# Graph attention on one core: masks turned two chunks at a time, statistics aggregated on GpSimd, another order at the end

## The reference

```python
h = maximum(layernorm(x), 0)                    # over the 256 features, eps 1e-5
Wh = h @ W                                      # 256 x 256
f1, f2 = Wh @ a[:256], Wh @ a[256:]
e = f1[:, :, None] + f2[:, None, :]
e = where(e >= 0, e, 0.2 * e)
att = softmax(where(adj > 0, e, -9e15), axis=1)
out = x + elu(einsum('bij,bjo->bio', att, Wh))
```

## Time and profile before

| | us |
|---|---|
| median of 3 runs | 989.29 |
| lowest, highest | 988.13, 992.64 |
| the profiled execution | 987.88 |
| its span | 986.1 |

### The profile page before, as it was taken

The page is one execution under the profiler, slowest core; times in us unless marked ns, Lnnn a source line. Parts: engine busy times, 40 slices in busy tenths (PEclk is TensorE's granted clock), DMA queues, the critical chain, the costliest instruction groups (busy, mean ns, idle before and its releaser), DMA issues.

```text
span 986.1 us, 23861 instructions
## 1 busy us (share of the span) xinstructions
PE 950.0 (96%) x8993; PEld 840.0 (85%) x8993; DVE 920.7 (93%) x1271; ACT 879.3 (89%) x1237; POOL 645.3 (65%) x676
## 2 busy tenths in 40 slices
PE   8878999999999999999999999999999999999996
PEld 6666888889888898888888888888988989898896
DVE  8799989999899998999989998999999999999975
ACT  4788989999999999999999899999999999898985
POOL 6567665776766776876767776677676775555540
PEclk8899999999999999999999999999999999999898
DMA  9477667889879889799979988979987978979724
GB/s 233 83 107 108 97 108 122 147 162 156 149 136 176 146 155 167 119 180 149 161 147 144 173 148 151 154 141 172 156 163 123 172 133 138 170 113 158 143 65 140
DMA packets 199093, 142.13 MB, mean 144 GB/s; under 512 B 7361, under 2 KB 187841, under 8 KB 198978
## 3 DMA queue, kind: packets, MB, share of 16 engines
q0 software_dynamic: 140160, 81.80, 61.5%
q1 hardware_dynamic: 58818, 58.81, 20.8%
HBM read 176.16 MB, written 16.84 MB: 196 GB/s over the span
## 4 chain that ended last, share of the span: by engine, by line
POOL 32%; PE 30%; issue 25%; DVE 5%; DMA 4%; ACT 2%; POOLq 0%; SPq 0%; DVEq 0%; ACTq 0%
POOL direct L896 10%; POOL xn L910 6%; POOL raw L882 5%; POOL inv L893 4%; PE acc L511 4%; PE acc L504 4%; PE acc L506 4%; PE tp L439 3%; PE acc_st L486 3%; PE acc_st L487 3%; PE acc_st L488 3%; POOL y L916 3%; PE pre L417 3%; POOL rstd L904 2%; POOL small_total L890 2%
## 5 line engine op out<-in xcount | busy, mean ns | idle before, releaser
L773 DVE CUSTOM_DVE_ANT_0 prob<-tp,f_row 128x2048 f32<-128x2048 bf16 x128 | 292.0, 2282 | 21.5 <-DMA f_row<-f_scratch 14.9
L590 ACT ACTIVATE prob<-prob,f 128x2049 f32<-128x2049 f32 x128 | 257.6, 2013 | 5.4 <-DVE prob L773 5.4
L486 PE MATMUL acc_st<-v,stored 128*128 128x256 f16 x960 | 261.5, 272 | 0.8 <-ACT part L620 0.8
L488 PE MATMUL acc_st<-v,stored 128*128 128x256 f16 x960 | 261.7, 273 | 0.0
L487 PE MATMUL acc_st<-v,stored 128*128 128x256 f16 x960 | 261.6, 273 | 0.0
L598 ACT ACTIVATE prob<-prob,shift 128x2048 f32<-128x2048 f32 x128 | 256.5, 2004 | 4.0
L896 POOL TENSOR_TENSOR direct<-prob,inv 128x1024 f16<-128x1024 f32 x128 | 243.5, 1902 | 10.0
L504 PE MATMUL acc<-v,direct 128*128 128x256 f16 x1024 | 233.4, 275 | 5.4 <-ACT z_direct L626 3.5
L506 PE MATMUL acc<-v,direct 128*128 128x256 f16 x1024 | 233.3, 274 | 0.0
L890 POOL TENSOR_SCALAR small_total<-total 128x1 f32<-128x1 f32 x128 | 29.8, 233 | 272.8 <-ACT prob L598 271.4
L604 ACT ACTIVATE stored<-prob,inv 128x1024 f16<-128x1024 f32 x128 | 146.1, 1142 | 47.6 <-POOL inv L893 47.6
(11 more groups left out here) (94 smaller groups left out, 1383.9 us busy)
## 6 DMA issues: line engine op xcount, KB each, us to landing
raw<-in_adj POOLq DMA_DIRECT2D x64, 1024.0 KB, 11.2
y<-in_x SPq DMA_DIRECT2D x63, 256.0 KB, 3.1
out<-y SPq DMA_DIRECT2D x63, 256.0 KB, 2.2
y<-elu POOLq DMA_DIRECT2D x56, 256.0 KB, 5.0
x_in<-in_x SPq DMA_DIRECT2D x108, 128.0 KB, 3.3
f_row<-f_scratch SPq DMA_DIRECT2D x31, 256.0 KB, 6.5
stored<-in_x SPq DMA_DIRECT2D x4, 512.0 KB, 6.9
f_scratch<-f_t SPq DMA_DIRECT2D x124, 0.5 KB
```

Of the source, the lines that this page charges most:

```text
L486: nc.tensor.matmul(bank[:, 0:FO], p_st[:, 0, rows], v_c[:, 0, :], start=(c == 0), stop=False)
L488: last = nc.tensor.matmul(bank[:, 0:FO], p_st[:, 1, rows], v_c[:, 0, :], start=False, stop=(c == G - 1))
L590: nc.scalar.activation(p_top, p_top, ACT.Prelu, bias=f2, alpha=ALPHA).then_inc(leaky, 1)
L773: nc.vector.tensor_tensor_reduce(out=prob[:, c % 2, 0:N], in0=tp_b, in1=f1_row[:, b % 2, :], scale=1.0, scalar=-3.0e38, op0=ALU.add, op1=A ...
```

## The change

1. **Masks.** `load_raw` brings one half of a pair's rows (even or odd rows) per DMA, so there are 128 DMAs of half the size, into four buffers. `make_masks` writes one byte per element, 192 where there is no edge, so that the bytes of two neighbouring columns form one 16-bit element. `transpose_masks` turns both chunks of a pair by sixteen transposes, in odd steps only. `mask_scores` reads every second byte of `tp` and subtracts `f1_row`, which carries a factor of 2^-48 that the operation's scale takes out again. Since neighbouring columns go to different chunks, the rows of `x` and of the output are taken in the same order: partition `p` holds rows 2p and 2p + 1.
2. **Statistics.** From chunk 20 on VectorE takes only `bn_stats`; `bn_aggr`, the eps and the offset go. GpSimd's `root_late` combines the even and odd statistics of four chunks in seven small operations of 4 columns ahead of the `pow`. `normalise` subtracts and multiplies; the missing factor of 2 is in the scale of ScalarE's rectifier.
3. **The end.** The second half of the last batch has no `store_block`. Its blocks 2 to 7 are summed in pairs in three banks by `last_blocks`: chunks 120 to 125 before the last chunk is done, the last two after it. VectorE adds the pairs (`add_last`) and copies half of the direct blocks and the extra ones. The nine last items have buffers of their own in `raw` and `neg`; their `x` is loaded in step 127. `x` is added by GpSimd for seven of them and by VectorE for two.

```diff
         raw = sb("raw", [P, 4, G, 2 * P], BF16)
+        neg_bytes = neg[:].rearrange("p b m j -> p b (m j)").bitcast(U8).rearrange("p b (t q j) -> p b t q j", t=2, q=G)
+        tp_bytes = tp[:].rearrange("p h c -> p (h c)").bitcast(U8).rearrange("p (i t) -> p t i", t=2)
...
+        def x_rows(c):
+            b, j = divmod(c, C)
+            q, t = divmod(j, 2)
+            return x[b, 2 * P * q:2 * P * (q + 1), :].rearrange("(p t) f -> t p f", t=2)[t]
...
+            def transpose_masks(pair):
+                pe.wait_ge(neg_ready, 2 * pair + 2)
...
+                wait(pe, scores, 2 * pair)
                 for m in range(C):
+                    last = nc.tensor.transpose(tp_b[:, m * P:(m + 1) * P], neg[:, pair % 2, m % 2 * G + m // 2, :],
+                                               ident_b[:])
...
+            def last_blocks(pair, chunks):
+                pe.wait_ge(lo_stored, chunks.stop)
...
+            last_blocks(2, range(SECOND, LAST - 1))
+            last_blocks(3, range(SECOND, LAST - 1))
+            direct_blocks(LAST)
+            extra_blocks(LAST - 1)
+            extra_blocks(LAST)
+            for pair in range(1, 4):
+                last_blocks(pair, range(LAST - 1, CH))
...
+            def make_masks(n):
+                pair, t = divmod(n, 2)
+                dve.wait_ge(raw_in[n % 4], 16 * (n // 4 + 1))
+                wait(dve, tp_ready, pair - 1)
+                nc.vector.tensor_scalar(neg_bytes[:, pair % 2, t], raw[:, n % 4], 0.0, NOT_AN_EDGE,
+                                        ALU.is_le, ALU.mult).then_inc(neg_ready, 1)
...
                 nc.vector.tensor_tensor_reduce(
-                    out=prob[:, c % 2, 0:N], in0=tp_b, in1=f1_row[:, b % 2, :], scale=1.0, scalar=-3.0e38,
-                    op0=ALU.add, op1=ALU.max, accum_out=prob[:, c % 2, N:N + 1]).then_inc(scores, 1)
+                    out=prob[:, c % 2, 0:N], in0=tp_bytes[:, c % 2, :], in1=f1_row[:, b % 2, :], scale=-1.0 / F1_SCALE,
+                    scalar=-3.0e38, op0=ALU.subtract, op1=ALU.max, accum_out=prob[:, c % 2, N:N + 1]).then_inc(scores, 1)
...
                     statistics(c)
-                    aggregate(c)
-                    if c == 0 or c % 4 == 3:
-                        add_eps(root_index(c))
+                    if c < EARLY:
+                        aggregate(c)
+                        if c == 0 or c % 4 == 3:
+                            add_eps(root_index(c))
...
+            def root_late(i):
+                chunks = root_group(i)
+                nth = i - root_index(EARLY) + 1
+                wait(pool, xn_ready, chunks.stop - RS)
+                rs = slice(chunks.start % RS, chunks.start % RS + 4)
+                pool.wait_ge(stats_s, chunks.stop)
+                mean, mean_odd, M, M_odd = (stats[:, rs, n] for n in (1, 4, 2, 5))
+                nc.gpsimd.tensor_tensor(agg[:, 0, :], mean, mean_odd, ALU.subtract).then_inc(sums_s, 1)
+                nc.gpsimd.tensor_tensor(agg[:, 1, :], M, M_odd, ALU.add).then_inc(sums_s, 1)
+                nc.gpsimd.tensor_tensor(offset[:, rs], mean, mean_odd, ALU.add).then_inc(sums_s, 1)
+                pool.wait_ge(sums_s, 3 * nth)
+                nc.gpsimd.tensor_tensor(agg[:, 0, :], agg[:, 0, :], agg[:, 0, :], ALU.mult).then_inc(square_s, 1)
+                nc.gpsimd.tensor_scalar(agg[:, 1, :], agg[:, 1, :], 4.0 / F, 4.0 * EPS, ALU.mult, ALU.add).then_inc(square_s, 1)
+                nc.gpsimd.tensor_scalar(offset[:, rs], offset[:, rs], 0.5, None, ALU.mult).then_inc(square_s, 1)
+                pool.wait_ge(square_s, 3 * nth)
+                nc.gpsimd.tensor_tensor(var_eps[:, rs], agg[:, 0, :], agg[:, 1, :], ALU.add).then_inc(scaled_s, 1)
+                pool.wait_ge(scaled_s, nth)
+                nc.gpsimd.tensor_tensor(rstd[:, rs], var_eps[:, rs], minus_half[:, 0:4], ALU.pow
+                                        ).then_inc(rstd_s, 1)
...
-                if s % 2 == 0 and s >= 0 and chunk(s + 4):
-                    load_raw(s // 2 + 2)
+                if s >= -1 and chunk(s + 5):
+                    load_raw(s + 5)
```

More of the change, by code:

```diff
@@ L157, in graph_attention @@
         y_ready = sem("y_ready")
+        y_ready_late = sem("y_ready_late")
+        x_last_in = [sem(f"x_last_in{i}") for i in range(NB + 1)]
+        last_done = sem("last_done")
+        z_last = sem("z_last")
+        z_direct_late = sem("z_direct_late")
         y_sum = [sem(f"y_sum{i}") for i in range(RY)]
@@ L211, in offset_at @@
                 return {-19: 2, -13: 3, -9: 4, -5: 5}[s]
-            g, late = divmod(s + 19, 4)
-            return g + 1 if late == 0 and EARLY // 4 <= g < CH // 4 else None
+            return None
         def root_at(s):
@@ L297, in graph_attention @@
                     finishing.append((b, i))
+        summed_by_dma = len(finishing)
+        finishing += [(B - 1, i) for i in LAST_ITEMS]
+        last_items = range(summed_by_dma, len(finishing))
+        summed_by_dve = len(finishing) - 2
         def single(k):
@@ L388, in _ @@
                 load_x(c)
-            for s in range(FIRST, END + 2):
+            for s in range(FIRST, CH + 1):
                 if chunk(s + 24) and s + 24 >= EARLY + RX:
@@ L403, in _ @@
                         read_f1((s + LEAD) // 4 - 1)
+            for k in last_items:
+                wait_for_y(sp, k)
+                sp.dma_start(rows_of(out, k), y_buf(k)).then_inc(y_out[k % RY], 16)
             for i in range(RY):
@@ L531, in extra_blocks @@
                 last.then_inc(extra_done, 1)
+            def last_blocks(pair, chunks):
+                pe.wait_ge(lo_stored, chunks.stop)
+                if chunks.start == SECOND:
+                    if pair == 1:
+                        pe.wait_ge(part_ready, firsts(SECOND - 1))
+                    else:
+                        pe.wait_ge(scores, CH)
+                for c in chunks:
+                    p_st = stored[:, c // G % 2, c % G]
+                    v_c = v[:, c % RV]
+                    for h in range(2):
+                        rows = slice((2 * pair + h) * P, (2 * pair + h + 1) * P)
+                        z = last_bank(pair)[:, h * FO:(h + 1) * FO]
+                        nc.tensor.matmul(z, p_st[:, 0, rows], v_c[:, 0, :], start=(c == SECOND and h == 0), stop=False,
+                                         skip_group_check=True)
+                        nc.tensor.matmul(z, p_st[:, 0, rows], v_c[:, 1, :], start=False, stop=False,
+                                         skip_group_check=True)
+                        last = nc.tensor.matmul(z, p_st[:, 1, rows], v_c[:, 0, :], start=False, stop=(c == LAST),
+                                                skip_group_check=True)
+                if chunks.stop == CH:
+                    last.then_inc(last_done, 1)
             pe.wait_ge(ident_f, 1)
@@ L547, in _ @@
                     make_wh(s + LEAD)
-            for s in range(END + 2):
+            for s in range(CH):
                 if chunk(s + LEAD):
@@ L555, in _ @@
                     store_block(n)
-                if chunk(s + 1):
-                    transpose_mask(s + 1)
+                if s == LAST:
+                    last_blocks(1, range(SECOND, LAST - 1))
+                if chunk(s + 1) and s % 2 == 1:
+                    transpose_masks((s + 1) // 2)
                 if chunk(s + LEAD + 1):
@@ L662, in _ @@
                     split_v_high(s + LEAD)
-            for s in range(END + 2):
-                batch_over = (s - 1) % C == 0 and 1 <= (s - 1) // C <= B
-                if batch_over:
+            for s in range(CH):
+                if (s - 1) % C == 0 and s > C:
                     take_direct((s - 1) // C - 1, 0)
@@ L841, in _ @@
                     multiply_w(3)
-                if offset_at(s) is not None and s >= 0:
-                    make_offset(offset_at(s))
-                if chunk(s + 2) and s >= 0:
-                    make_mask(s + 2)
+                for n in masks_at(s):
+                    make_masks(n)
                 if s == 0:
@@ L862, in _ @@
                     add_halves(n)
+            take_direct_late()
+            take_extra()
+            late = 1
+            for k in last_items:
+                finish_elu(k)
+                if late < 4:
+                    add_last(late)
+                    late += 1
         @block.gpsimd
@@ L941, in _ @@
                 if root_at(s) is not None:
-                    root(root_at(s))
+                    (root if root_at(s) < root_index(EARLY) else root_late)(root_at(s))
+            for k in range(summed_by_dma, summed_by_dve):
+                add_x(k)
 def kernel(x, adj, L0_gnn_W, L0_gnn_a):
```

261 lines of the change are left out of this document (145 added, 116 removed).

## The result

The changed kernel takes 1089.98 us, median of 4 runs (1087.12 to 1090.53), against 990.96 (988.13 to 994.96) for the kernel before: ratio 1.098, 95% interval 1.095 to 1.102. It is slower by 99 us; the forecast was 1003, and the end of its range 1034.

The account below looks back on a forecast made before the run. TensorE was taken to set the pace at 7.34 us a chunk, ScalarE's floor close behind at 7.19. Terms of -15 - 2 + 41 - 9.5 + 1 = +15.5 on 987.88 gave 1003 us, range 968 to 1034.

Parts of the forecast that it names:

- The bound and the floor: Mid-run, TensorE sets the pace at 7.34 us a chunk; ScalarE's own loop allows no less than 7.14 to 7.19.
- the -17 forecast: Packed transposes: 0.15 us a chunk gained over chunks 9 to 107, -15 us, and -2 in the last 20 chunks.
- The mask costs nothing directly: VectorE's byte mask takes 1.22 us, +0.50 a chunk, yet VectorE at 7.08 stays under ScalarE's 7.19.
- The cover: VectorE's margin under ScalarE's floor, 0.11 us a chunk, gone if the mask takes over 1.33 us.
- The statistics, +41: GpSimd's seven small operations, 2.15 us with waits, delay `small_total` and ScalarE in root steps, every fourth chunk: +41 us.
- The first root step of a batch, put at 0: At a batch's first chunk, 2.23 us of GpSimd idle time before `small_total` hides the small operations: delay 0.
- A missing term: the form of `normalise`: GpSimd's `normalise` changing to subtract and multiply: the prediction has no term for it.
- The parts were added as if apart: Whole kernel: terms for masks, statistics, end and rest were summed to +15.5 us.
- The rival of the shared port: VectorE holds GpSimd's small operations up in root steps, 1.5 us longer than forecast each: 1033 us, chance 0.08.
- The end, -9.5: After the last `mask_scores`: 13.3 us until the direct blocks, then 14.4, 27.7 in all instead of 37.1; -9.5 us.
- The signs to look for: New profile: transposes halved, TensorE under 95%, wait for `inv` about 75 us, mask about 1.2, end 28.
- three signs of being wrong: Small operations well under 0.2 us each, no growth in ScalarE's wait for `inv`, or VectorE without idle time.

Follow-up runs that it names:

- e13: e5 with the DMA casting masks to bytes and VectorE making two at once as 16-bit words; 969.3 us, ratio 0.977 to the kernel before.
- e5: The kernel before with the masks part of the change alone, statistics and end as before; 1004.0 us, ratio 1.013.
- e10: The changed kernel with GpSimd's small operations spread over three steps, x loaded earlier, and normalise as add and multiply; 1008.5 us, ratio 1.020.
- e6: The kernel before with the statistics part alone, two-byte masks and the old end; 1041.4 us, ratio 1.051.
- e16: The changed kernel with the mask operation on 16-bit words and nothing else changed; 1024.9 us, ratio 1.033 to the kernel before.
- e12: The kernel before with the new end alone, TensorE's direct blocks first, VectorE's three pair sums behind five items; 986.9 us, ratio 0.998.
- e4: Operations by themselves, no kernel's computation: GpSimd forms and VectorE's mask forms, other engine idle; normalise 1.227 us as subtract-multiply, 0.557 as add-multiply.

## Why the prediction was wrong

Two steps failed: the byte mask was taken to cost nothing, and the three parts were priced apart and added, though two of them lengthen work that VectorE and GpSimd hold each other up with. The term of the end failed too, and that of the statistics was too small.

- **The bound and the floor: borne out.** TensorE set the pace before. The floor of 7.14 to 7.19 us is where e13 runs, 7.14; that it is ScalarE's is likely, since its busy time and its wait for `inv` come to 7.08 there, but VectorE and TensorE are within 0.2 us. With a short mask the packing is worth more than the -17 forecast: -22 in e13.
- **"The mask costs nothing directly": failed.** Its own size was right (1.20 us at its quickest, 1.22 taken), and so was the byte read. But the sum took away the 0.30 us that the mask spent above its median, as if the holding up by GpSimd would end. It stayed: mean 1.42 against a median of 1.22 in e5, 1.64 in the kernel after. The cover was 0.11 us, and the term of -17 came out as +13. e5 keeps the aggregation, 0.18 us a chunk, on VectorE, which by the prediction's own sum puts VectorE at 7.26 there; but e10, which has it off VectorE, is no faster (1008.5), with the mask at 1.63 in mean.
- **The statistics, +41: path right, size wrong.** Alone they cost 50, with 100.0 us of waiting for `inv` between 100 and 900 us. The operations were taken at 0.23 and 0.29 and are 0.20 to 0.23. The `pow` was read as 1.63, 0.35 for each further column; alone it takes 1.04, so what it took above that was most likely holding up as well. But the holding up that the prediction kept for a rival ("seven short operations offer little to hold") came in every root step of the kernel after. The first root step of a batch, put at 0, was no exception: it grew by 2.6 us in e6.
- **A missing term: the form of `normalise`.** It was costed at nothing without a word. It costs 0 alone, 4 to 7 in the kernel after, 32 once the small operations are out of its way.
- **The parts were added as if apart: failed, 34 us.** The long byte operation holds `small_total` up (1.18 us above) and GpSimd holds it up in turn; e16 shows that most of the 34 us go with the byte mask, its operation and its DMA together. How they split is open: `small_total`, 0.39 us in mean against 0.31 in e6 and 0.25 in e16, makes up some 10, and `normalise`, 2.12 against 1.76 and 1.57, an unknown part. The rival of the shared port named the mechanism, and priced it at 1033 with a chance of 0.08.
- **The end, -9.5: failed, 0.** The term took the direct blocks at 13.3 us as before, though the diff puts 72 products ahead of them, and took no cost for GpSimd's sums. e12 got 2.6 us back.
- **The signs to look for:** transposes halved (136.1 to 68.1 us) and TensorE under 95%, right; wait for `inv` 75 us forecast, 132.9 measured; the end 28 forecast, 37.1 measured. TensorE's share, 87%, fell by the longer span as well. None of the three signs of being wrong came: they looked at cheap operations, at no wait, and at a VectorE without idle time, and not at operations that are held up.

The sum was -17 + 41 - 9.5 + 1; measured, by parts, it is +13 + 50 + 2 and 34 between them.

## What to carry to other kernels

Before work goes to an idle GpSimd, look at what VectorE runs at that moment: a 0.2 us operation can last as long as VectorE's instruction beside it, and a chain of them waits more than once. Where two parts of a change lengthen work on both of these engines, don't take it that their prices add, here they missed 34 us; undo each alone. Put such operations in several steps, and pick the form by a measurement of it alone. The best kernel here keeps the packed transposes, makes the masks on 16-bit words, has the reordered end, and leaves the statistics on VectorE or spreads them: 965 to 967 us, 2.5 to 2.7% under the kernel before.

## What the runs showed of the hardware that was not expected

On GpSimd, 128x256 in float32 with one scalar a partition for each operation, a pair with a subtraction takes 1.23 us (e4), one with an addition and a multiplication only 0.55 to 0.56, in either order; a single multiplication takes 0.93, more than the pair. The `pow` of four columns takes 1.04 us alone, where the kernel before shows 1.63.
